# Second pass: the two b2 products of a pair of tiles issued back to back, each on 64 rows

## The chip, the core and the metric

The kernel runs on one core of one Trainium2 chip. A core has five engines with instruction queues of their own: TensorE (PE; the records of its weight loads are kept apart as PEld), VectorE (DVE), ScalarE (ACT), GpSimd (POOL) and SyncE (SP, which here issues the DMAs). They meet through semaphores. The metric is the time on the device in microseconds (us) of the whole kernel; lower is better.

## The reference

One AdaLN transformer block over 8192 rows of 512 float32 numbers. First a linear attention with 16 heads of 32, then a mixture of 8 small experts, each stage behind a layernorm that is scaled and shifted by a modulation vector:

```python
h = _layernorm(x) * (1 + ca) + sa
q, k = elu(h @ Wq.T + bq) + 1, elu(h @ Wk.T + bk) + 1        # 16 heads of 32
KV = einsum('bhsd,bhsm->bhmd', k, v); Z = 1 / (q . sum(k) + 1e-6)
x = x + ga * ((q KV Z) @ Wo.T + bo)
h = _layernorm(x) * (1 + cb) + sb
V = h @ fWv.T + fbv
s = _ln(V @ Wg.T + bg) + sigmoid(alpha) * _ln(norms of the probes Wp V)
w = softmax over the two best of the 8 scores s              # 0 for the other six
delta = sum_e w_e * (silu(V @ W1[e].T + b1[e]) @ W2[e].T + b2[e])
x = x + gb * (V + delta)
```

The term that the change touches is the sum over e of w_e * b2[e]. For each row it is a product of the 8 router weights with an 8 x 512 matrix.

## The kernel before

The 8192 rows are 64 tiles of 128 rows. All large products are float32 products split into a high and a low part in the type float32r: a_hi b_hi + a_hi b_lo + a_lo b_hi. The helper `three` issues them (the lines L1475, L1476 and L1480 of the profile), always with 128 x 128 stationary values and 328 or 512 moving columns.

The **first pass** goes over single tiles (normalise, turn, K and Q products, the sum of k times the normalised x). The **second pass** goes over 32 pairs of tiles; `sweep_pairs(step_b, -1, J + 1)` with J = 32 is a pipeline that is written out by hand in the same way for every engine. In step j TensorE runs, in this order: the fused products of pair j-1 (`c_hi`, `c_lo`), the attention output products of pair j (`g_hi`, `g_lo`) with the turns of the hidden values of pair j-2 between and behind them, the two expert products of pair j-2, and the value products of pair j-1 (`v_hi`, `v_lo`) with the turns of x2 of pair j. No scheduler moves anything: the order in the code is the order on the engine.

The names around the change:

- `ws` (128 x 128) holds the router weights of both tiles of a pair, h = 0 and h = 1. VectorE writes them into 64 columns for each h: the rounded weights in columns 64h to 64h+7, what the rounding left in 64h+8 to 64h+15, and the rounded weights again in 64h+32 to 64h+39. The other columns stay zero. TensorE turns `ws` once for each pair (`turn_hidden` with h = 0), and ScalarE copies the result to `wT_hi`. In `wT_hi` the weights of tile h stand on partitions 64h to 64h+39.
- `b2st` (128 x 2 x 512) is made once. `b2st[:, h, :]` holds b2 (with the value bias and gb folded in) on the matching partitions of half h, and zeros on the 64 partitions of the other half.
- `bank_y(h)` is one PSUM bank of 128 x 512 for each tile. `value_product` starts it, `expert_product` adds the b2 product and six products of the hidden values (`aT_hi`, `aT_lo` with `w2_hi`, `w2_lo`) and then signals `y_psum`.
- `aTh_done` says that ScalarE has written `aT_hi` (and for h = 0 `wT_hi` as well), `aTl_done` that VectorE has written `aT_lo`. VectorE's `finished` waits for `y_psum`, adds the residual and frees the bank.

Of the kernel before, what the change touches and what calls it, by code (L numbers as in the profile page):

```python
# [29 lines left out]
P = 128  # L30
# [81 lines left out]
def build(nc, x, Wq, bq, Wk, bk, Wv, bv, Wo, bo, fWv, fbv, Wg, bg, Wp, alpha, g_r, b_r, g_c, b_c,  # L112
# [13 lines left out]
    with ctx:  # L126
        def sb(name, shape, dt=F32, stack=ctx):
            return stack.enter_context(nc.sbuf_tensor(name, shape, dt))
# [11 lines left out]
        half = sb("half", [P, 2 * E])  # L140
# [39 lines left out]
        b2st = sb("b2st", [P, 2, D], F32R)  # L180
# [85 lines left out]
        wT_hi = sb("wT_hi", [P, P], F32R, late)  # L266
# [152 lines left out]
        def bank_y(h):  # L419
            return ps[:, h, :]  # L420
# [1046 lines left out]
        def _(pe):  # L1467
# [3 lines left out]
            def three(dst, parts, start, stop, low_ready=None, n_low=0):  # L1471


                for n, (ah, al_, bh, bl) in enumerate(parts):
                    nc.tensor.matmul(dst, ah, bh, start=start and n == 0, stop=False)  # L1475
                    nc.tensor.matmul(dst, ah, bl, start=False, stop=False)  # L1476
                if low_ready is not None:
                    pe.wait_ge(low_ready, n_low)
                for n, (ah, al_, bh, bl) in enumerate(parts):
                    last = nc.tensor.matmul(dst, al_, bh, start=False, stop=stop and n == len(parts) - 1)  # L1480
                return last
# [44 lines left out]
            for b in range(KB):  # L1526
                pe.wait_ge(wma_in[b], 16)
                for v in range(2):
                    last = nc.tensor.matmul(ps[:, v, :], c_col[:, 2, b:b + 1].to_broadcast([P, P]), wm_in[:, v, b, :],  # L1529
                                            start=(b == 0), stop=(b == KB - 1))  # L1530
# [120 lines left out]
            def expert_product(j, h):  # L1651
                t = 2 * j + h
                pe.wait_ge(aTh_done, t + 1)
                nc.tensor.matmul(bank_y(h), wT_hi[:], b2st[:, h, :], start=False, stop=False)  # L1654
                three(bank_y(h), [(aT_hi[:, h, b * P:(b + 1) * P], aT_lo[:, h, b * P:(b + 1) * P],
                                   w2_hi[:, b, :], w2_lo[:, b, :]) for b in range(2)], False, True,
                      aTl_done, t + 1).then_inc(y_psum, 1)
# [21 lines left out]
            def step_b(j):  # L1679
# [21 lines left out]
                if live(j - 2, J):  # L1701
                    turn_hidden(j - 2, 1)
                    expert_product(j - 2, 0)
                    expert_product(j - 2, 1)
# [40 lines left out]
```

## Time and profile before

| | us |
|---|---|
| median of 3 runs | 1246.58 (1246.37 to 1248.93) |
| the profiled execution | 1246.3 |
| its span, first to last instruction | 1244.6 |
| TensorE busy in the span | 1218.9 |
| mean granted TensorE clock | 0.994 of 2.4 GHz |

A row of the profile names a line, an engine, an operation, the tiles written and read, the shape and a count. A matmul and the load of its stationary values are two records (MATMUL on PE, LDWEIGHTS on PEld). The end of a matmul is modelled, and records of successive matmuls overlap, so the distance from one start to the next tells what a matmul takes from the engine, and the recorded duration does not. "idle" is the time in which an engine had no record, and the arrow names what ended it.

### The profile page before, as it was taken

The page shows a single profiled execution, that of the slowest core. Times are in us where ns is not written, and L with a number is a line of the kernel's source. Part 1 is how long each engine was busy: PE and PEld are TensorE (multiplying, and loading weights), DVE is VectorE, ACT ScalarE, POOL GpSimd, SP SyncE. Part 2 cuts the span into 40 slices and gives each one's busy share as a digit, 9 for nine tenths or more (in the row PEclk, how much of TensorE's full clock was granted, in tenths as well). Part 3 has the DMA queues.
Part 4 walks back from the last instruction along what each step waited for, and adds up shares of the span by engine and source line. Part 5 has one row for each costly group of instructions (what it writes and reads, how often), then busy time and mean ns, then how long its engine had stood idle before and what let it go on. Part 6 is the DMA issues. An engine that isn't in the chain of part 4 may idle for free.

```text
span 1244.6 us, 18483 instructions
## 1 busy us (share of the span) xinstructions
PE 1218.9 (98%) x5742; PEld 1002.0 (81%) x5742; DVE 996.9 (80%) x2275; ACT 537.8 (43%) x1117; POOL 547.8 (44%) x401
## 2 busy tenths in 40 slices
PE   8999999999999999999699999999999999999998
PEld 5788878787877787888478888888888888888887
DVE  5877778988889988876778888888788878888865
ACT  2444444454444554454333434434434343443431
POOL 1344343433343433332454644646546455464531
PEclk9999999999999999999899999999999999999999
DMA  8556444444343443442413323223132231322201
GB/s 208 164 156 200 153 137 140 142 138 125 106 133 101 136 129 109 136 126 67 105 43 93 91 63 102 66 88 101 52 103 71 82 102 52 102 76 78 86 19 50
DMA packets 131681, 131.64 MB, mean 106 GB/s; under 512 B 12328, under 2 KB 86480, under 8 KB 131584
## 3 DMA queue, kind: packets, MB, share of 16 engines
q1 hardware_dynamic: 131584, 130.47, 34.3%
q8 instruction: 46, 0.75, 0.3%
q14 instruction: 51, 0.42, 0.1%
HBM read 80.62 MB, written 49.81 MB: 105 GB/s over the span
## 4 chain that ended last, share of the span: by engine, by line
PE 88%; DVE 5%; ACT 3%; issue 2%; DMA 1%; POOL 0%; SPq 0%; DVEq 0%; ACTq 0%; POOLq 0%
PE ps L1475 27%; PE ps L1476 27%; PE ps L1480 27%; PE ps L1662 3%; PE ps L1654 1%; PE ps L1568 1%; DVE zk L1201 1%; DMA wm_in<-in_L_wmod_dram 1%; PE ps L1529 1%; ACT exp_k L805 1%; DVE qf L1184 1%; ACT exp_k L807 0%; ACT exp_q L798 0%; ACT exp_q L800 0%; PE ps L1625 0%
## 5 line engine op out<-in xcount | busy, mean ns | idle before, releaser
L705 POOL TENSOR_TENSOR cn<-c,half 128x16 f32<-128x16 f32 x32 | 104.2, 3256 | 257.4 <-DVE c L1338 257.4
L667 POOL TENSOR_TENSOR xn_lo<-xn,xn_hi 128x512 fp32r<-128x512 f32 x64 | 85.6, 1338 | 278.0 <-ACT xn_hi L780 278.0
L1475 PE MATMUL ps<-g_hi,qT_hi 128*128 128x512 f32 x256 | 104.8, 409 | 4.9 <-ACT qT_hi L843 4.9
L798 ACT ACTIVATE exp_q<-qf 128x512 f32<-128x512 f32 x64 | 40.4, 632 | 157.0 <-DVE qf L1184 157.0
L1475 PE MATMUL ps<-wk_hi,xT_hi 128*128 128x512 f32 x256 | 102.0, 398 | 2.4 <-ACT xT_hi L774 2.4
L1475 PE MATMUL ps<-wq_hi,xT_hi 128*128 128x512 f32 x256 | 102.4, 400 | 0.5 <-DVE wq_lo L1006 0.5
L1475 PE MATMUL ps<-v_hi,xT_hi 128*128 128x512 f32 x256 | 102.9, 402 | 0.0
L1475 PE MATMUL ps<-k_hi,xn_hi 128*128 128x512 f32 x256 | 102.3, 400 | 0.0
L1476 PE MATMUL ps<-g_lo,qT_hi 128*128 128x512 f32 x256 | 101.6, 397 | 0.0
L1476 PE MATMUL ps<-wq_lo,xT_hi 128*128 128x512 f32 x256 | 101.4, 396 | 0.0
L1476 PE MATMUL ps<-wk_lo,xT_hi 128*128 128x512 f32 x256 | 101.3, 396 | 0.0
L1476 PE MATMUL ps<-k_lo,xn_hi 128*128 128x512 f32 x256 | 100.7, 393 | 0.0
L1476 PE MATMUL ps<-v_lo,xT_hi 128*128 128x512 f32 x256 | 100.2, 391 | 0.0
L1480 PE MATMUL ps<-k_hi,xn_lo 128*128 128x512 f32 x256 | 100.1, 391 | 0.0
L672 POOL TENSOR_TENSOR ks_acc<-ks_acc,zk 128x512 f32<-128x512 f32 x64 | 88.1, 1376 | 4.6 <-DVE zk L1213 4.6
L836 ACT CAST xT_hi<-ps 128x512 fp32r<-128x512 f32 x64 | 37.5, 587 | 107.4 <-PE ps L1662 107.4
L679 POOL TENSOR_TENSOR xb<-xin,bo_ga 128x1024 f32<-128x1024 f32 x32 | 77.7, 2427 | 9.4 <-DMA xin<-_attn_hidden_states_dram 9.2
L1475 PE MATMUL ps<-c_hi,xT_hi 128*128 128x328 f32 x256 | 80.8, 324 | 0.0
L697 POOL TENSOR_TENSOR qks<-q_in,ks_q 128x1024 f32<-128x1024 f32 x32 | 76.9, 2404 | 8.1 <-DMA q_in<-q_scratch 8.1
L805 ACT ACTIVATE exp_k<-zk 128x512 f32<-128x512 f32 x64 | 40.6, 634 | 87.9 <-DVE zk L1201 87.8
L1476 PE MATMUL ps<-c_lo,xT_hi 128*128 128x328 f32 x256 | 78.0, 315 | 0.0
L662 POOL TENSOR_TENSOR rstd<-veps,neg_half 128x1 f32<-128x1 f32 x64 | 44.7, 698 | 73.2 <-DVE veps L948 72.7
(240 smaller groups left out, 3293.2 us busy)
## 6 DMA issues: line engine op xcount, KB each, us to landing
xin<-_attn_hidden_states_dram SPq DMA_DIRECT2D x64, 256.0 KB, 3.1
q_scratch<-qf SPq DMA_DIRECT2D x64, 256.0 KB, 3.3
xin<-_attn_hidden_states_dram SPq DMA_DIRECT2D x32, 512.0 KB, 4.2
q_in<-q_scratch SPq DMA_DIRECT2D x128, 128.0 KB, 2.9
out_dram<-qf SPq DMA_DIRECT2D x64, 256.0 KB, 2.0
xn_scratch<-xn SPq DMA_DIRECT2D x62, 256.0 KB, 2.1
xq<-xn_scratch SPq DMA_DIRECT2D x248, 64.0 KB, 2.4
wm_in<-in_L_wmod_dram SPq DMA_DIRECT2D x4, 1024.0 KB, 5.8
```

The costliest lines, as they stand in the source:

```text
L662: nc.gpsimd.tensor_tensor(rstd[:, s:s + 1], veps[:, s:s + 1], neg_half[:, 0:1], ALU.pow).then_inc(rstd_done, 1)
L667: nc.gpsimd.tensor_tensor(quarters(xn_lo[:, 1 - s, :]), natural(xn[:, 1 - s, :]), quarters(f32(xn_hi[:, 1 - s, :])), ALU.subtract).then_in ...
L672: nc.gpsimd.tensor_tensor(ks_acc[:], ks_acc[:], kf[:, s, :], ALU.add).then_inc(ks_done, 1)
L679: nc.gpsimd.tensor_tensor(xb[:], xin[:], bo_ga[:].unsqueeze(1).to_broadcast([P, 2, D]), ALU.add).then_inc(xb_done, 1)
L697: nc.gpsimd.tensor_tensor(qks[:].rearrange("p h (g f) -> p (h g) f", f=P), q_of(j).rearrange("p (n f) -> p n f", f=P), ks_q[:].unsqueeze(1 ...
L705: nc.gpsimd.tensor_tensor(cn[:].rearrange("p h e -> p (h e)"), c2[:].rearrange("p h e -> p (h e)"), half[:], ALU.pow).then_inc(cn_done, 1)
L798: nc.scalar.activation(exp_q[:, 1 - s, :], zq[:, 1 - s, :], ACT.Relu, scale=-1.0).then_inc(rq_done, 1)
L805: nc.scalar.activation(exp_k[:, s, :], zk[:, s, :], ACT.Relu, scale=-1.0).then_inc(rk_done, 1)
L836: nc.scalar.copy(xT_hi[:, h, :], bank_x2T).then_inc(x2Th_done, 1)
L1475: nc.tensor.matmul(dst, ah, bh, start=start and n == 0, stop=False)
L1476: nc.tensor.matmul(dst, ah, bl, start=False, stop=False)
L1480: last = nc.tensor.matmul(dst, al_, bh, start=False, stop=stop and n == len(parts) - 1)
```

## The change

`expert_product` of the tile h = 0 now issues the b2 products of both tiles, one behind the other. Each of them reads 64 partitions of `wT_hi` and `b2st` in place of all 128: the product of tile 0 partitions 0 to 63, that of tile 1 partitions 64 to 127. `expert_product` of h = 1 issues none. What each bank receives is the same sum, since the partitions left out hold zeros.

```diff
             def expert_product(j, h):
                 t = 2 * j + h
                 pe.wait_ge(aTh_done, t + 1)
-                nc.tensor.matmul(bank_y(h), wT_hi[:], b2st[:, h, :], start=False, stop=False)
+                if h == 0:
+                    for g in range(2):
+                        half = slice(g * P // 2, (g + 1) * P // 2)
+                        nc.tensor.matmul(bank_y(g), wT_hi[half, :], b2st[half, g, :], start=False, stop=False)
                 three(bank_y(h), [(aT_hi[:, h, b * P:(b + 1) * P], aT_lo[:, h, b * P:(b + 1) * P],
                                    w2_hi[:, b, :], w2_lo[:, b, :]) for b in range(2)], False, True,
                       aTl_done, t + 1).then_inc(y_psum, 1)
```

On TensorE, in the second pass, the rows around the two expert products of one pair stood like this before (`ident,aw` is the turn of the hidden values of tile 1, L1654 the b2 product):

```order
 L1662 MATMUL ps<-ident,aw 128x128 x2
 L1654 MATMUL ps<-b2st,wT_hi 128x512
 L1475 MATMUL ps<-w_hi,aT_hi 128x512
 L1476 MATMUL ps<-w_lo,aT_hi 128x512
 L1475 MATMUL ps<-w_hi,aT_hi 128x512
 L1476 MATMUL ps<-w_lo,aT_hi 128x512
 L1480 MATMUL ps<-w_hi,aT_lo 128x512 x2
 L1654 MATMUL ps<-b2st,wT_hi 128x512
```

The same place with the change, where the lines of the turn and the b2 product are L1665 and L1657 (the shape printed is that of the output, so the 64 partitions don't show in it):

```order
 L1665 MATMUL ps<-ident,aw 128x128 x2
 L1657 MATMUL ps<-b2st,wT_hi 128x512 x2
 L1475 MATMUL ps<-w_hi,aT_hi 128x512
 L1476 MATMUL ps<-w_lo,aT_hi 128x512
 L1475 MATMUL ps<-w_hi,aT_hi 128x512
 L1476 MATMUL ps<-w_lo,aT_hi 128x512
 L1480 MATMUL ps<-w_hi,aT_lo 128x512 x2
 L1475 MATMUL ps<-w_hi,aT_hi 128x512
```

The b2 product of tile 1 has moved ahead of the six products of tile 0. The count of instructions is the same, and the order on VectorE, ScalarE, GpSimd and SyncE is unchanged.

## Rows read from the trace of the kernel before

**Rows 1.** The page: span, and the chain that ended last, by engine.
```profile
span 1244.6 us, 18483 instructions
...
PE 88%; DVE 5%; ACT 3%; issue 2%; DMA 1%; POOL 0%; SPq 0%; DVEq 0%; ACTq 0%; POOLq 0%
```

**Rows 2.** Busy time by stretch: first pass, second pass, its end (columns in the first row).
```profile
core 0: us, PE busy (x) PEld busy (x) DVE busy (x) ACT busy (x) POOL busy (x), PEclk, DMA share, GB/s
0.00:640.00 640.00, 618.57 (x2663) 490.99 (x2664) 514.28 (x918) 297.72 (x512) 242.56 (x222) 0.99 0.44 133
640.00:1200.00 560.00, 560.00 (x2863) 476.48 (x2862) 459.63 (x1276) 229.81 (x577) 296.51 (x173) 1.00 0.26 80
1200.00:1244.60 44.60, 40.31 (x221) 34.54 (x218) 23.02 (x83) 10.26 (x28) 8.71 (x6) 0.99 0.10 36
```

**Rows 3.** The b2 product's own line: duration ns min/median/max, first and last start.
```profile
L1654 PEld LDWEIGHTS ps<-b2st,wT_hi x64: 187/188/190, 648.3 to 1239.3; 128*128 128x128 f32 x64
L1654 PE MATMUL ps<-b2st,wT_hi x64: 395/436/478, 648.4 to 1239.5; 128*128 128x512 f32 x64
```

**Rows 4.** The chain in one pair: start us, us that each step added, line.
```profile
899.13 0.94 PE ps L1480 x4
900.07 0.22 PE ps L1662 x2
900.29 0.23 PE ps L1654
900.52 0.23 PE ps L1475
...
901.45 0.47 PE ps L1480 x2
901.92 0.23 PE ps L1654
902.15 0.23 PE ps L1475
```

**Rows 5.** Timeline of TensorE in that pair: start us, recorded length us.
```profile
899.91 0.38 PE L1662 MATMUL ps<-ident,aw 128*128 128x128 f32 x2
900.04 0.48 PE L1654 MATMUL ps<-b2st,wT_hi 128*128 128x512 f32 x1
900.36 0.39 PE L1475 MATMUL ps<-w_hi,aT_hi 128*128 128x512 f32 x1
900.59 0.40 PE L1476 MATMUL ps<-w_lo,aT_hi 128*128 128x512 f32 x1
```

**Rows 6.** Timeline of the weight loads there.
```profile
900.02 0.19 PEld L1654 LDWEIGHTS ps<-b2st,wT_hi 128*128 128x128 f32 x1
900.13 0.19 PEld L1475 LDWEIGHTS ps<-w_hi,aT_hi 128*128 128x128 f32 x1
900.36 0.19 PEld L1476 LDWEIGHTS ps<-w_lo,aT_hi 128*128 128x128 f32 x1
```

**Rows 7.** The chain at the end of the last pair.
```profile
1236.26 0.23 PE ps L1662 x2
...
1237.53 0.14 issue
1237.66 0.41 PE ps L1662 x2
1238.07 0.23 PE ps L1654
...
1241.37 0.69 DVE qf L1347
```

**Rows 8.** What VectorE waited for from 660 to 1200 us: total us, times, longest us.
```profile
DVE qf L1347 <- PE ps L1480: 23.4, 29, 0.9
```

**Rows 9.** Timeline of ScalarE and VectorE there: when the hidden values are ready.
```profile
900.33 0.37 ACT L857 CAST aT_hi<-ps 128x256 fp32r<-128x256 f32 x1 [0.41 <-PE ps L1662]
900.73 0.42 DVE L1326 TENSOR_TENSOR aT_lo<-ps,aT_hi 128x256 fp32r<-128x256 f32 x1
```

## The prediction

> **What bounds the kernel now.** I read the busy time by stretch first. From 640 to 1200 us TensorE has a record in all 560.00 of 560 us, at a granted clock of 1.00, while VectorE has 459.63 and no other engine more than 296.51 [rows 2]. The chain that ended last lies on PE for 88% of the span of 1244.6 us [rows 1]. So in the second pass nothing releases TensorE but its own queue: whatever time its instructions take more or less goes into the end, unless another engine becomes late. The reader should then look at the chain inside one pair [rows 4]. Each 512-column product adds 0.23 us, the two turns ahead of the b2 product add 0.22 together, and the b2 product is a step like any other, although only half of its rows hold anything.
>
> Two facts beside this decide the case. First, the record of a product lasts 0.39 to 0.40 us, but the next one starts 0.23 us behind it (900.36 and 900.59) [rows 5]. So about 0.395 - 0.2325 = 0.16 us of every product lies under its successor; 0.2325 is seven such steps of the chain, 900.29 to 901.92, divided by seven [rows 4]. Second, the weights of a product are loaded while its predecessor runs: the load for the product at 900.36 starts at 900.13, and two loads in a row stand 0.11 us apart (900.02, 900.13) [rows 6].
>
> **The change, part by part.** It concerns 64 b2 products in 32 pairs [rows 3], all of them on TensorE's path.
>
> *The move.* The b2 product of tile 1 goes ahead of the six products of tile 0. Moving it alone costs TensorE nothing: it needs `wT_hi`, which tile 0 needs as well, and a bank that TensorE itself wrote in the step before. What follows on TensorE and waits is the first product of tile 1 (for `aT_hi`), due at about 901.92; even if the two b2 products took the time of one it is due at 901.7, and ScalarE is done at 900.70 and VectorE with `aT_lo` at 901.15 [rows 9]. So no wait comes up. VectorE waits for the sum of tile 0 in `finished`, 23.4 us in 29 times or 0.8 us each [rows 8]. If nothing overlaps, that sum is ready up to 0.23 us later and this wait grows to 1.0 us; queued behind it are the sums over qks and the second `finished`, but VectorE has 100 us of idle time in 560 [rows 2], about 3 us in each pair, which covers it. I cost the move at 0.
>
> *The 64 rows.* The trace has no product on fewer than 128 rows, so I bound the effect from both sides for one pair. Before, the two products take 2 x 0.2325 = 0.465 us.
>
> The best end: the two products work on different rows, write different banks and run beside each other, and the engine passes between shapes freely. They then take one step, 0.2325 us: a gain of 0.2325 us. If the second must wait for its own weights, loaded 0.11 us behind the first's [rows 6], the pair takes 0.34 and the gain is 0.12. Over 32 pairs that is -7.4 to -3.9 us.
>
> The worst end: the engine must be empty when it goes from 128 rows to 64 and again when it goes back. Then the 0.16 us that lie under the successor come to light at two borders, one behind the turns and one ahead of the first `w_hi` product. If the weights can't be loaded before it is empty either, each border costs a load as well. The nearest rows for this are two: the spacing of two loads, 0.11 us [rows 6], and the restart in the last pair, where two turns behind an idle time add 0.41 us in place of 0.23, so 0.18 more [rows 7]. The pair would take 0.16 + 0.11 + 0.2325 + 0.16 + 0.11 = 0.77 us with the smaller load, and 0.16 + 0.18 + 0.34 + 0.16 + 0.18 = 1.02 with the larger one and the second product held back by its own load. Against 0.465 that is +0.31 to +0.56 us, over 32 pairs +9.8 to +17.8.
>
> Between them: the engine empties at both borders, but the weights are loaded meanwhile, as they are beside every running product in [rows 6]. The pair takes 0.16 + 0.2325 + 0.16 = 0.555 us, which is 0.09 more than 0.465: over 32 pairs +2.9 us. This is the value that I take. The weight load is the part for which the rows speak plainly; that the two products run beside each other is what different rows and banks allow; and the two borders are the part for which I have no row, only the amount, 0.16, that is at stake in each.
>
> The trace has one switch of mode that costs nothing: from turns to products the chain goes on without a gap (0.22 for two turns, then 0.23) [rows 4]. That speaks for the cheap end, but both sides of it use all 128 rows. The Trainium skill (TensorEngine Tiling (Array Packing), Key Properties) says that changing the tiling mode, in contrast to changing the tile, drains TensorE. No run here shows it yet; by that rule the sum lies at +2.9 us or above, and without it at -3.9 or below.
>
> **The rivals.**
>
> *A, overlap with free borders: faster.* One mechanism: the product of tile 1 starts while that of tile 0 runs, on the other half of the rows. It decides from the point where the two starts stand closer than 0.2325 us less what the borders cost. For it speaks the free switch between turns and products [rows 4]; against it, that the weights of two products have to be loaded in the 0.22 us of the turns. Its time is 1246.3 - 7.4 to 1246.3 - 3.9, so 1238.9 to 1242.4 us. The Trainium skill (TensorE: Matmul & The Clock Gate, Part 3, The mechanism) describes this overlap, with starts about 4 ns apart; by that the gain would be at its larger end, 7.3 us.
>
> *B, drain at both borders with the weights already loaded: my forecast.* 1246.3 + 2.9 = 1249.2 us. Since the ends of matmuls are modelled, the part under the successor may be smaller than the records say: with 0.10 us at a border the pair takes 0.43 and gains 1.0 us in all; with 0.22 it loses 6.6. Its own range is 1245.3 to 1252.9.
>
> *C, drain with the loads exposed, or without overlap of the two products: clearly slower.* 1246.3 + 9.8 to + 17.8, so 1256.1 to 1264.1. Drain with loaded weights and no overlap gives 0.16 + 0.465 + 0.16, so +0.32 us in a pair and 1256.5, the same place. For it speaks that TensorE has nothing else to run in the gap; against it, that loads run ahead everywhere.
>
> *D, it doesn't do what it says: no change.* The two products follow each other like full ones at 0.23 us, and the borders are free: 1246.3 us.
>
> **How the numbers follow.** The profiled execution took 1246.3 us, 1.7 more than its span; the median of the runs shown is 1246.58, 0.3 above it, so I add 0.3. Chances: B 0.36, A 0.30, C 0.22, D 0.12. B gives 1249.5. Differences under 0.2%, 2.5 us, can't be told from no change. Faster by more than that is A and a small end of B: 0.31. Same is D and the part of B between a gain of 1.0 and a loss of 2.5: 0.23. Slower is the rest of B and C: 0.46. The range reaches from the smaller gain of A and some of the way to its larger one, 1241.3, up to the lower end of C, 1258. Within B alone it is 1245.6 to 1253.2.
>
> **What the changed profile would show.** The timeline around one pair tells all: the starts of the two b2 products, 0.23 us apart if they don't overlap (C or D), 0.11 or less if they do. The distance from the last turn to the first b2 product, and from the second one to the first `w_hi` product, tells the borders: under B about 0.16 us more than now at each, under C also weight loads that start only after the engine is empty. In all cases the other products keep 0.23 us, the clock stays at 1.00 and the first pass up to 640 us keeps its length. From the first turn of `aw` to the first product of tile 1, the chain would grow by 0.09 us under B, and shrink by 0.12 to 0.23 under A. I am wrong if the borders are free (the time falls under 1243), if the loads are exposed (it rises over 1256), or if a new wait of TensorE for VectorE or ScalarE shows up in the second pass.

## The result and the profile after

The changed kernel takes 1250.92 us in the median of 13 runs (1250.1 to 1254.57); the kernel before took 1247.21 in 13 runs beside it (1245.35 to 1249.13). The ratio is 1.0034, 95% interval 1.0026 to 1.0043: slower by 4.2 us, from 3.2 to 5.4 (the two medians lie 3.7 apart). The profiled execution took 1252.12 us with a span of 1250.4. That is 5.8 us more than the profiled execution before, of which 0.7 had been lost before the first b2 product began (649.1 us in place of 648.4), ahead of all code that the change touches.

The page still calls TensorE busy 98% of the span and puts the same 88% of the chain on it [rows 1]:

```profile
span 1250.4 us, 18483 instructions
...
PE 88%; DVE 5%; issue 3%; ACT 3%; DMA 1%; POOL 1%; SPq 0%; DVEq 0%; ACTq 0%; POOLq 0%
```

The second pass by stretch (columns as in [rows 2]) shows no idle TensorE either: 560.00 of 560 us, at the same clock. But it holds fewer of its instructions, 2839 in place of 2863: the pairs have become longer.

```profile
640.00:1200.00 560.00, 560.00 (x2839) 468.31 (x2839) 444.39 (x1263) 227.99 (x576) 294.02 (x172) 1.00 0.25 79
```

The b2 product's own line answers to [rows 3] (duration ns min/median/max, first and last start). Its shape is now 64 rows, and its records last 498 ns, 62 more in the median than before:

```profile
L1657 PEld LDWEIGHTS ps<-b2st,wT_hi x64: 182/183/184, 649.1 to 1243.7; 64*128 64x128 f32 x64
L1657 PE MATMUL ps<-b2st,wT_hi x64: 492/498/502, 649.1 to 1243.7; 64*128 64x512 f32 x64
```

The chain in one pair, to be laid beside [rows 4]:

```profile
901.81 0.94 PE ps L1480 x4
902.75 0.22 PE ps L1665 x2
902.96 0.43 PE ps L1657 x2
903.39 0.43 PE ps L1475
903.82 0.23 PE ps L1476
...
904.52 0.47 PE ps L1480 x2
904.99 0.23 PE ps L1475
```

Here the time of a step is the distance between the ends of successive records. Both b2 products together add 0.43 us where one full product added 0.23, and the first `w_hi` product behind them adds 0.43 as well, where it used to add 0.23. That is 0.86 us for what were three steps of 0.2325, 0.70 us. All other steps are as before. So a pair has grown by 0.16 us, and 32 pairs by 5.2 us. The first b2 product of a pair tells the same over the whole pass: from 649.1 to 1243.7 us there are 31 pairs of 19.18 us, before from 648.4 to 1237.83 31 of 19.01.

Where the 0.16 us come from shows in the timelines of TensorE and of its weight loads [rows 5, 6]:

```profile
902.58 0.38 PE L1665 MATMUL ps<-ident,aw 128*128 128x128 f32 x2
902.89 0.50 PE L1657 MATMUL ps<-b2st,wT_hi 64*128 64x512 f32 x2
903.32 0.50 PE L1475 MATMUL ps<-w_hi,aT_hi 128*128 128x512 f32 x1
903.66 0.40 PE L1476 MATMUL ps<-w_lo,aT_hi 128*128 128x512 f32 x1
```

```profile
902.58 0.14 PEld L1665 LDWEIGHTS ps<-ident,aw 128*128 128x128 f32 x1
902.89 0.19 PEld L1657 LDWEIGHTS ps<-b2st,wT_hi 64*128 64x128 f32 x2 [0.17 <-issue]
903.32 0.19 PEld L1475 LDWEIGHTS ps<-w_hi,aT_hi 128*128 128x128 f32 x1 [0.24 <-issue]
903.43 0.19 PEld L1476 LDWEIGHTS ps<-w_lo,aT_hi 128*128 128x128 f32 x1
```

Three things are to be seen. The two b2 products fill 0.50 us together, which is what one record alone lasts (498 ns): they start within 0.01 us of each other and run beside each other, and so do their loads.

The load for them starts at 902.89. By then the two turns have been fed in for 0.09 us (902.58 + 2 x 0.11 = 902.80). Before, the load started 0.02 ahead of its product's record, beside the turns.

And the load for `w_hi` waits as well. The record of a product at a border begins together with its load and is 0.10 us longer than the 0.395 of an unhindered one. So I take it that the b2 products are fed from about 902.995 (the record's end, 903.39, less 0.395) for one step of 0.2325, to 903.23. The load for `w_hi` starts at 903.32, 0.09 us behind that, and again some 0.10 to 0.11 us pass before its product goes.

So each border costs 0.20 us: 0.09 in which nothing is fed or loaded, which I read as the engine emptying, and 0.11 for a weight load that nothing covers. The 0.20 is the chain's; its two parts rest on the modelled ends of the records and are an estimate. The sum is 0.20 + 0.2325 + 0.20 = 0.63 us for a pair, against 0.465.

The busy share can't show this, since the modelled ends of the records cover the gaps. The idle time of the weight loads can. Over 660 to 1200 us (total us, times, longest us):

```profile
DVE qf L1347 <- PE ps L1480: 34.2, 29, 1.2
...
PEld ps L1475 <- issue: 6.8, 28, 0.2
PEld ps L1657 <- issue: 4.7, 28, 0.2
```

Each border stands there once in a pair, and neither had a row before. The first row answers to [rows 8]: VectorE waits 1.2 us for the sum of tile 0, it was 0.8. TensorE in turn waits for no other engine from 640 us up to the last pair.

### The profile page after: what moved, and what is told of

Its sections match the earlier page's. It is cut to its first block, busy times and chain, and to the rows that moved or that the text cites. A ratio compares the mean times of both kernels' runs of the same rounds, so it can differ in the third digit from the quotient of the medians.

```text
span 1250.4 us, 18483 instructions
## 1 busy us (share of the span) xinstructions
PE 1222.9 (98%) x5742; PEld 996.2 (80%) x5742; DVE 986.0 (79%) x2275; ACT 537.8 (43%) x1117; POOL 547.8 (44%) x401
## 4 chain that ended last, share of the span: by engine, by line
PE 88%; DVE 5%; issue 3%; ACT 3%; DMA 1%; POOL 1%; SPq 0%; DVEq 0%; ACTq 0%; POOLq 0%
PE ps L1475 27%; PE ps L1476 27%; PE ps L1480 26%; PE ps L1665 3%; PE ps L1657 1%; PE ps L1568 1%; DVE zk L1201 1%; DMA wm_in<-in_L_wmod_dram 1%; PE ps L1529 1%; ACT exp_k L805 1%; DVE qf L1184 1%; ACT exp_k L807 0%; ACT exp_q L798 0%; ACT exp_q L800 0%; PE ps L1521 0%
```

## The experiments

All are read by the same chain in one pair, and each diff is against the kernel before unless it says otherwise. The kernel before took 1247.23 us beside the first four (15 runs), 1247.08 beside the others (21 runs).

**The order alone.** Both products moved together, with their 128 rows.

```diff
-                nc.tensor.matmul(bank_y(h), wT_hi[:], b2st[:, h, :], start=False, stop=False)
+                if h == 0:
+                    for g in range(2):
+                        nc.tensor.matmul(bank_y(g), wT_hi[:], b2st[:, g, :], start=False, stop=False)
```

> The order of the change with the shape of before: both b2 products back to back, each on all 128 rows. Theory 1 (the loss comes from passing between 128-row and 64-row work, two borders in each pair of about 0.20 us, of which the overlap gives back 0.23): no border, so no change, ratio within 0.2% of before, and the chain in a pair adds 0.23 us for each b2 product and for the first w_hi product. Theory 2 (the loss comes from the new order, because the sum of tile 0 is ready later and VectorE or a semaphore holds TensorE): as slow as the change, ratio about 1.0034.

Measured: 1246.35 us, ratio 0.9995 (0.9986 to 1.0004). The order costs nothing; theory 2 is out. The chain keeps its steps:

```profile
900.47 0.22 PE ps L1664 x2
900.69 0.46 PE ps L1656 x2
901.15 0.23 PE ps L1475
```

**The shape alone.** 64 rows each, at the old places.

```diff
-                nc.tensor.matmul(bank_y(h), wT_hi[:], b2st[:, h, :], start=False, stop=False)
+                half = slice(h * P // 2, (h + 1) * P // 2)
+                nc.tensor.matmul(bank_y(h), wT_hi[half, :], b2st[half, h, :], start=False, stop=False)
```

> The shape of the change in the order of before: each b2 product reads 64 rows, but stands at the head of its own tile's products. That makes four borders in a pair and no overlap. Theory 1 (border 0.20 us, overlap complete): 4 x 0.20 = 0.80 us more in a pair, over 32 pairs +25 us, about 1272 us. Theory 3 (the two products in the change do not really overlap, and a border costs only about 0.08 us, which gives the same measured 0.16 us in a pair less the missing 0.23): 4 x 0.08 = 0.33 us in a pair, +10.6 us, about 1257 us. Theory 2 (order): no change.

Measured: 1271.0 us, ratio 1.0197 (1.0183 to 1.0211), so +24.6 us, or 0.77 us in a pair for four borders: 0.19 each. That is theory 1; theory 3, with its 0.08, is out. The chain shows the second pair of borders standing behind 512-column products just as the first stands behind the turns:

```profile
909.87 0.22 PE ps L1663 x2
910.09 0.43 PE ps L1655
910.52 0.43 PE ps L1475
...
911.65 0.46 PE ps L1480 x2
912.11 0.42 PE ps L1655
912.53 0.43 PE ps L1475
```

**Overlap made impossible.** Both products on rows 0 to 63.

```diff
-                nc.tensor.matmul(bank_y(h), wT_hi[:], b2st[:, h, :], start=False, stop=False)
+                if h == 0:
+                    for g in range(2):
+                        nc.tensor.matmul(bank_y(g), wT_hi[0:P // 2, :], b2st[0:P // 2, g, :], start=False, stop=False)
```

> As the change, but both b2 products read rows 0 to 63, so the two can not run beside each other (the b2 part of tile 1 is left out: its rows there are zeros). Theory 1: the overlap is lost and the borders stay, so the pair grows by one step of 0.2325 us against the change, over 32 pairs +7.4 us, about 1258 us; the starts of the two products lie 0.23 us apart. Theory 3 (there was no overlap in the change): the same time as the change, about 1251 us.

Measured: 1260.49 us, ratio 1.0109 (1.0095 to 1.0123), 9.4 us more than the change against their kernels before, with an uncertainty of some 2 us. The chain gives the size more sharply: the two products add 0.66 us in place of 0.43, and the border behind them is the same.

```profile
907.88 0.22 PE ps L1664 x2
908.10 0.66 PE ps L1656 x2
908.76 0.43 PE ps L1475
```

0.23 us in 32 pairs are 7.4 us. In the profiled execution the second pass also began later (first b2 product at 651.1 us, with the change at 649.1), ahead of all edited code. The clock tells why. From 20 to 30 us, in the preparation, TensorE was granted a mean of 0.83 of 2.4 GHz in the profile of the change and 0.66 in this one (columns as in [rows 2], the change first): its clock stood at 1.2 GHz until some 25.4 and 28.4 us, and the eight products there, L1521, took 5.32 and 6.75 us.

```profile
20.00:30.00 10.00, 7.88 (x20) 4.47 (x21) 7.51 (x16) 3.56 (x6) 0.61 (x1) 0.83 0.59 150
20.00:30.00 10.00, 7.77 (x14) 3.69 (x15) 6.08 (x14) 2.56 (x4) 0.61 (x1) 0.66 0.58 142
```

So the overlap in the changed kernel is real, and worth a whole step.

**The pair twice.** Against the change:

```diff
-                    for g in range(2):
+                    for g in (0, 1, 0, 1):
                         half = slice(g * P // 2, (g + 1) * P // 2)
                         nc.tensor.matmul(bank_y(g), wT_hi[half, :], b2st[half, g, :], start=False, stop=False)
```

> As the change, but the two b2 products are issued twice, rows 0, 64, 0, 64 (b2 is counted twice). This adds a second 64-row pair without another border. Theory 1: inside 64-row work a pair costs one step of 0.2325 us, so +7.4 us against the change, about 1258 us. If each product waits for its own weight load inside 64-row work, 0.34 us for the second pair, +10.9 us, about 1262. If there is no overlap at all, 0.465 us, +14.9 us, about 1266.

Measured: 1260.68 us, ratio 1.0112 (1.0098 to 1.0126), 9.7 us more than the change. By the time alone this lay between the first two cases of the expectation. The chain settles it: four products add 0.67 us, so the second pair took 0.24, one step; the rest is again the later begin (651.0 us, with the same 0.66 from 20 to 30 us).

```profile
908.11 0.67 PE ps L1657 x4
908.77 0.43 PE ps L1475
```

**Three pairs on 64 rows, and the same work on 128.** The loop above with `(0, 1, 0, 1, 0, 1)`, once with `half` and once with all rows; the diff leads from the first to the second:

```diff
-                        nc.tensor.matmul(bank_y(g), wT_hi[half, :], b2st[half, g, :], start=False, stop=False)
+                        nc.tensor.matmul(bank_y(g), wT_hi[:], b2st[:, g, :], start=False, stop=False)
```

> The b2 pair of the change three times in a row (six 64-row products, rows 0, 64, 0, 64, 0, 64; b2 is counted three times). Theory 1 (a border costs 0.20 us once on each side, inside 64-row work a pair costs one step): 2 x 0.235 us more in a pair than the change, +15 us, about 1266 us; the chain adds 0.43 + 0.47 us for the six and 0.43 for the first w_hi product. Rival: a cost of its own in each pair inside 64-row work (the second pair cost 9.7 us in the times before, 7.5 by the chain): +19 us, about 1270.

> The counterpart of it on all 128 rows: six full b2 products in a row, no border, no overlap (b2 is counted three times). Theory 1: 4 x 0.2325 us more in a pair than before, +29.8 us, about 1277 us, so 11 us slower than the same work in three 64-row pairs: the overlap is real and pays once the stretch is long enough, by 5 x 0.2325 - (0.20 + 0.20 + 2 x 0.235) = 0.29 us in a pair. If the overlap were not real, this kernel would be the faster one of the two, by the borders.

Measured: 1267.78 us on 64 rows (ratio 1.0161, 1.0145 to 1.0177) and 1276.22 on 128 (1.0234, 1.0219 to 1.0248). The rival with an extra cost in each 64-row pair is out: three pairs cost 0.90 us in the chain, two steps of 0.235 more than one. And with six products the 64-row form is the faster one, by 8.4 us. The same two borders are paid, but three steps are given back and not one. The chain on 64 rows, then on 128:

```profile
890.09 0.22 PE ps L1665 x2
890.31 0.90 PE ps L1657 x6
891.20 0.43 PE ps L1475
```

```profile
890.88 0.22 PE ps L1664 x2
891.10 1.40 PE ps L1656 x6
892.49 0.23 PE ps L1475
```

**104 rows.**

```diff
-                nc.tensor.matmul(bank_y(h), wT_hi[:], b2st[:, h, :], start=False, stop=False)
+                if h == 0:
+                    for g in range(2):
+                        nc.tensor.matmul(bank_y(g), wT_hi[0:104, :], b2st[0:104, g, :], start=False, stop=False)
```

> As the order of the change, but both b2 products read rows 0 to 103, which hold all the router weights of both tiles (only zero rows are left out). If the border belongs to the shape into which the array is divided (128 rows in one piece, or two pieces of 64), 104 rows still need the undivided array and nothing changes: ratio within 0.2% of before, chain 0.23 us for each step. If any product on fewer rows than its neighbours has the border: two borders of 0.20 us and no overlap, +12.8 us, about 1260 us.

Measured: 1247.52 us, ratio 1.0000 (0.9991 to 1.0009). So 104 rows bring no border; the loads start ahead again (898.76, with the product's record at 898.79).

```profile
898.82 0.22 PE ps L1664 x2
899.04 0.46 PE ps L1656 x2
899.50 0.24 PE ps L1475
```

**Half the columns.** The change with 256 columns in each b2 product; the diff is against the change.

```diff
-                        nc.tensor.matmul(bank_y(g), wT_hi[half, :], b2st[half, g, :], start=False, stop=False)
+                        nc.tensor.matmul(bank_y(g)[:, 0:D // 2], wT_hi[half, :], b2st[half, g, 0:D // 2],
+                                         start=False, stop=False)
```

> As the change, but each b2 product covers 256 of the 512 columns (b2 is left out for the other half). Theory 1 (both products stream at the same time, the borders don't depend on the columns): the pair streams 256 columns less, 0.11 us, so -3.4 us against the change, about 1248 us, still no gain against before although half of the b2 work is gone. If the products streamed one behind the other, -6.8 us, about 1244.5 us. If a border grows with the length of the product ahead of it: less than 1247.

Measured: 1248.09 us, ratio 1.0005 (0.9996 to 1.0014), no difference from before that can be told by the times. The pair adds 0.32 us in place of 0.43, and 0.11 us is the time of 256 columns once; had the products followed each other, it would be twice that. The step behind it stays at 0.43: the border doesn't depend on the columns, and even half of the b2 work in this form does not gain on all of it in the old one.

```profile
901.78 0.22 PE ps L1666 x2
902.00 0.32 PE ps L1657 x2
902.32 0.43 PE ps L1475
```

**The times at an equal clock.** The executions of one kernel differ by up to 5 us, and the difference goes with the mean granted clock of the execution. A straight line through 102 executions (36 of the kernel before, those of the change and of all experiments) gives 0.95 us for each 0.001 of the mean clock. At an equal clock the distances from the kernel before are, as an estimate with some 0.5 us to either side:

| | by the times at an equal clock, us | by the chain, 32 pairs, us |
|---|---|---|
| the change | +6.1 | +5.2 |
| order alone | +0.1 | 0 |
| shape alone | +25.9 | +25 |
| overlap made impossible | +13.0 | +12.6 |
| the pair twice | +13.6 | +12.9 |
| three pairs | +20.7 | +20.2 |
| six products on 128 rows | +30.5 | +29.8 |
| 104 rows | +0.2 | 0 |
| half the columns | +2.0 | +1.7 |

With that, the 9.4 and 9.7 us that the overlap made impossible and the pair twice cost beyond the change become 6.9 and 7.5, beside 7.4 and 7.7 by the chain. The 4.2 us of the change become 6.1: 7 of its 13 executions were at 0.996, and none of the 36 of the kernel before was above 0.995. Between 5 and 6 us is what the traces and the times together allow for it. Half the columns comes out a little slower than before, as by the chain.

## Why the prediction was right, and where it was not

*The bound.* Right: the second pass is TensorE's, and every 0.01 us of a pair went into the end 32 times.

*The move costs nothing.* Right, shown by the order alone (0.9995). With the order alone VectorE's wait for the sum of tile 0 is the 1.0 us that I named (29.6 us in 29 times); with the change it grew to 1.2, because the borders delay that sum too. Its idle time covered it, as I had argued. One reading was off without harm: by [rows 4] the first product of tile 1 was due at 902.15, or 901.92 with the overlap, and not at 901.92 and 901.7, which leaves more room still.

*The two products run beside each other.* Right, and fully: one step for two, shown by taking the overlap away (0.66 in place of 0.43 us) and by repeating the pair (0.24 us for each further one). My fear that the second would stand behind its own load, 0.11 us, did not come true: the two loads start together as well.

*The two borders.* That TensorE loses time at each border, the first half of my forecast B, is what happens; the row that I laid against it, the free switch between turns and products [rows 4], says nothing on it, since both use all 128 rows. The Trainium skill (TensorEngine Tiling (Array Packing), Key Properties) has this rule, a drain when the mode changes and not when the tile changes, and the runs here agree: 0.20 us at a border, nothing inside 64-row work or on 104 rows. That the gap is an emptying is the rule's word; the traces show the gap and its length.

*What a border is made of* is the step that failed. I took 0.16 us for the emptying, from the part of a record that lies under its successor, and nothing for the load, and called the load "the part for which the rows speak plainly". It was the other way round: the emptying takes about 0.09 us, less than the modelled records say, and the load of 0.11 us is exposed at both borders. Exposed loads were what I had named as a sign of being wrong, with a time over 1256; the sign came, the time did not. [Rows 6] show loads ahead only inside one shape; I carried them across a change of shape without a row for it. That the forecast of 1249.5 us is near the 1250.92 measured is therefore in part luck. The two errors nearly cancel: B's 0.16 became 0.20 at a border, +0.09 us in a pair became +0.16, and +2.9 us became +5.2 by the chain and 4.2 (3.2 to 5.4) in the times. With the exposed load of C and the smaller end of my bounds for the emptying, 0.10 + 0.11 at a border, the sum would have come to 0.65 us for a pair, +6 us.

*The rivals.* A needs free borders, and its overlap alone is true; with them it would have gained 7.4 us. C had the exposed load but too long an emptying: its 0.16 + 0.11 at a border would have made +9.8 us. D, no overlap and free borders, is out by the chain of the shape alone and of the overlap made impossible.

*Not settled:* why the load isn't started while the engine empties. The traces show only that it isn't. Nor was two pairs in one stretch laid against four full products; by the chain they should win (0.20 + 0.20 + 2 x 0.235 = 0.87 us against 0.93), and shown in the times is only the win of three. This kernel has one pair of b2 products for two banks, and no version here beats the kernel before.

## What to carry to other kernels

In this kernel two products on different halves of the rows do run in the time of one, but going over from 128-row work to 64-row work and back costs 0.40 us, 1.7 steps of 512 columns; a single pair loses, three pairs in one stretch win, and two should by the chain's numbers. Count the borders, not the rows: 104 rows cost the same as 128, and only the 64-row products brought borders. And a load that runs ahead in every row of a trace does so between instructions of one kind; before crossing into another shape, reckon also with the case that it is exposed.

## What the runs showed of the hardware that I had not expected

Between 128-row and 64-row work a weight load starts only about 0.09 us after the work before it has been fed in, so its 0.11 us are added in full. The weight loads of two products on different halves start at the same moment (two in 0.19 us, which is the length of one). And a TensorE that is called busy for 560.00 of 560 us can hide 0.40 us of gaps in every 19.2: it takes the idle rows of the weight loads, or the steps of the chain, to see them.
